# Scores of the first batch element by fp32 matmuls on 32 rows, straight from T

## The reference

```python
Q = einsum('oc,bscm->bsom', Wq, x) + bq      # o = 256 hidden channels
K = einsum('oc,bscm->bsom', Wk, x) + bk
V = einsum('oc,bscm->bsom', Wv, x) + bv
QK = Q^T @ K  over s                           # 256 x 256 for each element and lane
A  = softmax(QK, axis=-1)
out = einsum('bmcC,bmsC->bsCm', A, V)        # only the column sums of A enter
y  = x + Wo out + bo
```

## Time and profile before

| | |
|---|---|
| time, median of three | 199.22 us (196.81 to 209.14) |
| time of the profiled execution | 199.71 us |
| its span | 197.9 us |
| mean granted TensorE clock | 0.911 |
| busy: PE, DVE, ACT, POOL | 165.7, 130.8, 128.8, 99.5 us |
| first exponential of element 0, of element 1 | 31.99 us, 51.63 us |
| first instruction of the last chain after the exponentials | 185.43 us |

### The profile page before, as it was taken

The page is one execution under the profiler, slowest core; times in us unless marked ns, Lnnn a source line. Parts: engine busy times, 40 slices in busy tenths (PEclk is TensorE's granted clock), DMA queues, the critical chain, the costliest instruction groups (busy, mean ns, idle before and its releaser), DMA issues. The chain is left out here.

```text
span 197.9 us, 5954 instructions
## 1 busy us (share of the span) xinstructions
PE 165.7 (84%) x2208; PEld 89.7 (45%) x2208; DVE 130.8 (66%) x291; ACT 128.8 (65%) x529; POOL 99.5 (50%) x122
## 2 busy tenths in 40 slices
PE   0697096999897899999999999989897898799753
PEld 0263035555454545564545455535454453464330
DVE  0355429748886788778777878788778766654241
ACT  0200005957798688788868887988798998874401
POOL 3353656404897299497558755963642303214000
PEclk9999758569999999999999999999999999955975
DMA  5900585893299169639933972588079502200202
GB/s 192 365 6 0 108 196 96 199 239 146 31 199 252 66 131 205 210 62 197 260 137 58 208 206 81 76 196 264 12 128 215 201 0 109 103 6 0 106 5 106
DMA packets 9626, 26.61 MB, mean 134 GB/s; under 512 B 2459, under 2 KB 3326, under 8 KB 9598
## 3 DMA queue, kind: packets, MB, share of 16 engines
q1 hardware_dynamic: 8224, 25.57, 50.1%
q10 hardware_dynamic: 1374, 0.67, 1.3%
HBM read 9.06 MB, written 4.19 MB: 67 GB/s over the span
## 5 line engine op out<-in xcount | busy, mean ns | idle before, releaser
L772 ACT ACTIVATE e_sb<-s_bank,negmax 128x256 f32<-128x256 f32 x256 | 117.6, 495 | 49.6 <-DVE negmax L584 27.9
L584 DVE TENSOR_REDUCE negmax<-s_bank 128x2 f32<-128x512 f32 x128 | 87.1, 686 | 24.4 <-PE s_bank L404 23.1
L404 PE MATMUL s_bank<-stack,wq_st 99*128 99x256 f32 x256 | 63.2, 341 | 3.7 <-ACT e_sb L772 2.5
L404 PEld LDWEIGHTS s_bank<-stack,wq_st 99*128 99x128 f32 x256 | 39.8, 201 | 41.0 <-issue 40.7
L772 ACT ACTIVATION_READ_ACCUMULATOR e_sb<-s_bank,negmax 128x1 f32 x256 | 58.1, 227 | 0.0
L414 PE MATMUL acc<-e_sb,recip 128*32 128x256 f32 x512 | 43.4, 412 | 9.4 <-DVE recip L590 8.9
L815 POOL TENSOR_TENSOR xc<-xs,nm 128x512 f32<-128x512 f32 x15 | 15.9, 1082 | 20.1 <-DVE nm L543 20.1
L866 POOL TENSOR_TENSOR t_parts<-t_sb,t_parts 128x1280 fp32r<-128x1280 f32 x7 | 20.4, 2908 | 4.3 <-DVE t_parts L579 3.8
L565 DVE SCALAR_TENSOR_TENSOR t_sb<-bk_sb,ssum,bz 128x256 f32<-128x256 f32 x28 | 12.9, 465 | 12.4 <-PE bz L382 10.4
L879 POOL TENSOR_TENSOR ws<-wo_sb,aT 128x1024 f32<-128x1024 f32 x7 | 13.4, 1912 | 14.2 <-DVE aT L600 14.2
L414 PEld LDWEIGHTS acc<-e_sb,recip 128*32 128x32 f32 x512 | 10.7, 111 | 20.8 <-DVE recip L590 13.8
(11 more groups left out here) (72 smaller groups left out, 128.8 us busy)
## 6 DMA issues: line engine op xcount, KB each, us to landing
stack<-t_parts SPq DMA_DIRECT2D x32, 256.0 KB, 4.9
xs<-x_rows SPq DMA_DIRECT2D x8, 512.0 KB, 5.7
stack<-t_parts SPq DMA_DIRECT2D x32, 128.0 KB, 4.8
xT<-x_cols SPq DMA_DIRECT2D x8, 512.0 KB, 6.0
y_cols<-yb SPq DMA_DIRECT2D x7, 512.0 KB, 4.1
y_cols<-yb SPq DMA_DIRECT2D x2, 256.0 KB, 2.0
stack<-t_parts SPq DMA_DIRECT2D x8, 32.0 KB
k_sb<-consts ACTq DMA_DIRECT2D x1, 235.5 KB, 4.5
```

Of the source, the lines that this page charges most:

```text
L404: mm = nc.tensor.matmul(s_bank[p % NS][:, CH * h:CH * h + CH], wq_st[:, P * h:P * h + P], stack[:, side, p % Q, p // Q, :], start=True, st ...
L584: nc.vector.tensor_reduce(negmax[:, p % NS, :], s_bank[p % NS][:, :].rearrange("p (h n) -> p h n", h=HC), op=ALU.max, axis=AX.X, negate=Tr ...
L772: last = nc.scalar.activation(e_sb[:, p % NE, h, :], s_bank[p % NS][:, CH * h:CH * h + CH], ACT.Exp, bias=negmax[:, p % NS, h:h + 1], accu ...
```

## The change

Elements 1 to 7 get their scores as before. Element 0 no longer goes through `high_part`, `low_part` and the stack: its scores are fp32 matmuls on the 32 rows of a lane in `t_sb`, with the plain weights `wq_sb` (a new load of 128 KB), and a second matmul on 12 rows adds the bias: `bq_rows` (split bq, picked per t, made by POOL from `bq_sb`, another new load of 128 KB) times `tb_st` (split bias rows in all 128 partitions). Two halves that lie in different row blocks and PSUM banks are issued together: half 1 of lane p and half 0 of lane p + 1. T of element 1 is computed in slots 1 to 5 of element 0, no longer ahead of it, and the statistics of elements 2 and 3 come later too. `gnorm` and `ssum` get two buffers.

```diff
-ANCHOR = {2: 7, 3: 22, 4: 36, **{j: M * (j - 2) + 3 for j in range(5, B)}}
+ANCHOR = {0: 0, 1: 1, 2: 13, 3: 24, 4: 37, **{j: M * (j - 2) + 3 for j in range(5, B)}}
+NEVER = -1000
+HI_FIRST, SPLIT_WQ = 6, 9
 EARLY = {
-    2: {**CHAIN, **dict(gram=-7, variance=-4, read_gram=-6, sum_diagonal=-5, read_variance=-3)},
-    3: {**CHAIN, **dict(sum_rows=-17, mean=-14, gram=-10, sum_groups=-16, read_mean=-13)},
-    4: {**CHAIN, **dict(sum_rows=-18, mean=-15, sum_groups=-17, read_mean=-14)},
+    0: {**dict.fromkeys(CHAIN, NEVER), **dict(t23_product=0, read_t2=0, read_t3=1)},
+    1: {**dict.fromkeys(CHAIN, NEVER), **dict(t01_product=0, tb_product=1, t23_product=3,
+                                              read_t0=1, read_t1=2, read_tb=2, read_t2=3, read_t3=4)},
+    2: {**CHAIN, **dict(sum_rows=-11, mean=-9, gram=-6, variance=-4, sum_groups=-11, read_mean=-9,
+                        read_gram=-5, sum_diagonal=-4, read_variance=-3)},
+    3: {**CHAIN, **dict(sum_rows=-13, mean=-11, gram=-9, variance=-5, sum_groups=-12, read_mean=-10,
+                        read_gram=-7, sum_diagonal=-6, read_variance=-4)},
+    4: {**CHAIN, **dict(sum_rows=-16, mean=-13, gram=-10, sum_groups=-15, read_mean=-12, read_gram=-8, sum_diagonal=-7)},
+    5: {**CHAIN, **dict(sum_rows=-18, sum_groups=-17)},
 }
...
+            def tb_product_first():
+                pe.wait_ge(sblk_done, 1)
+                nc.tensor.matmul(by[:, 0:CH], sblk_first[:, :, :, :].rearrange("p q k t -> p (q k t)"), wk_sb[:, :],
+                                 start=True, stop=True).then_inc(tb_mm, 1)
+
+            def score_first(halves):
+
+                for p, h in halves:
+                    t, q = p // Q, p % Q
+                    pe.wait_ge(t_read, t + 1)
+                    after(pe, exped, p - NS + 1)
+                    rows = slice(C * q, C * q + C)
+                    nc.tensor.matmul(s_bank[p % NS][:, CH * h:CH * h + CH], wq_sb[rows, P * h:P * h + P],
+                                     t_sb[rows, 0, t, :], start=True, stop=False)
+                for p, h in halves:
+                    t, q = p // Q, p % Q
+                    rows = slice(C * q, C * q + NP * T)
+                    mm = nc.tensor.matmul(s_bank[p % NS][:, CH * h:CH * h + CH], bq_rows[rows, t, P * h:P * h + P],
+                                          tb_st[rows, :], start=False, stop=True)
+                    if h == HC - 1:
+                        mm.then_inc(scores, 1)
+
             def score(b, p):
+                if b == 0:
+                    score_first([(p, 1), (p + 1, 0)] if p + 1 < M else [(p, 1)])
+                    return
...
-            sum_rows(2)
-            pe.wait_ge(w_loaded, 16 * 7)
+            pe.wait_ge(w_loaded, 16 * 8)
             t_product(0, 0, t01_mm, bz)
-            tb_product(0)
-            t_product(0, 2, t23_mm, t23_bank(0))
+            tb_product_first()
             gram_of(1)
-            mean(2)
+            pe.wait_ge(bq_done, 1)
+            pe.wait_ge(tb_split, 2)
+            score_first([(0, 0)])
+            score(0, 0)
+            score(0, 1)
             variance(1)
-            t_product(1, 0, t01_mm, bz)
-            tb_product(1)
-            t_product(1, 2, t23_mm, t23_bank(1))
-            pe.wait_ge(set_dve, 2)
-            for p in range(AHEAD):
-                score(0, p)
+            score(0, 2)
```

More of the change, by code:

```diff
@@ L81, in shape_constants, with build @@
     k[p, PAIR + p // (2 * C)] = 1.0
+    k[p % C // T == 1, BLO] = -1.0
+    k[p % C // T == 2, TLO] = -1.0
+    for t in range(T):
+        k[p % C == 0 * T + t, PICKT + t] = 1.0
+        k[p % C == 1 * T + t, PICKT + t] = 1.0
+        k[p % C == 2 * T + t, PICKT + t] = 1.0
     return k
-def build(nc, x_rows, x_cols, wq_stack, wk_rep, bk_rep, wv, wo, bv, bo_rep, consts, y_cols):
+def build(nc, x_rows, x_cols, wq_stack, wq_rep, bq_rep, wk_rep, bk_rep, wv, wo, bv, bo_rep, consts, y_cols):
     f32 = mybir.dt.float32
@@ L112, in build @@
         wk_sb = sb("wk_sb", [P, CH])
+        wq_sb = sb("wq_sb", [P, CH])
+        bq_sb = sb("bq_sb", [P, CH])
+        bq_hi = sb("bq_hi", [P, CH], f32r)
+        bq_st = sb("bq_st", [P, CH], f32r)
+        bq_rows = sb("bq_rows", [P, T, CH], f32r)
         bk_sb = sb("bk_sb", [P, CH])
@@ L280, in bias @@
                     sp.dma_start(dst.bitcast(f32), src.bitcast(f32)).then_inc(bias_stacked[side], 16)
[L282 to L298, removed]
+                for q in range(Q):
+                    high(q)
+                bias(0)
+                sp.wait_ge(parts_done, j)
+                bias(1)
+                for q in range(Q):
+                    low(q)
             def store(j):
@@ L306, in _ @@
                 load_rows(j)
-            stack_up(0)
+            load_cols(0)
             stack_up(1)
-            load_cols(0)
             for b in range(B):
@@ L381, in t_product @@
                         rows = slice(C * q, C * q + C)
-                        mm = nc.tensor.matmul(dst[rows, CH * i:CH * i + CH], gnorm[rows, first + i, :],
+                        mm = nc.tensor.matmul(dst[rows, CH * i:CH * i + CH], gnorm[rows, j % 2, first + i, :],
                                               wk_sb[rows, :], start=True, stop=True)
@@ L412, in column_sums @@
                         after(pe, acc_read, b)
+                    if b == 0 and t == 0:
+                        pe.wait_ge(vare_done, 2)
                 for q in range(Q):
@@ L638, in element @@
                         invert(n // T, n % T)
+                    if slot == HI_FIRST:
+                        high_part(1)
+                    if slot == SPLIT_WQ:
+                        split_wq()
                     if b >= 3 and p == 0:
@@ L900, in _ @@
             column_means(1)
-            pool.wait_ge(w_loaded, 16 * 7)
-            for h in range(HC):
-                last = nc.gpsimd.tensor_scalar(wobv[:, h], wo_sb[:, h, :], bv_sb[:, h:h + 1], 0.0, ALU.mult, ALU.add)
-            last.then_inc(set_pool, 1)
             diagonal(1)
@@ L908, in _ @@
             scaled_sums(1)
+            pool.wait_ge(w_loaded, 16 * 8)
+            for h in range(HC):
+                last = nc.gpsimd.tensor_scalar(wobv[:, h], wo_sb[:, h, :], bv_sb[:, h:h + 1], 0.0, ALU.mult, ALU.add)
+            last.then_inc(set_pool, 1)
             centre_rows(2)
             column_means(2)
+            diagonal(2)
             low_part(1)
-            diagonal(2)
             power(2)
```

158 lines of the change are left out of this document (93 added, 65 removed).

## The result

The changed kernel takes 216.68 us, the median of four runs (215.91 to 217.10), against 200.3 for the kernel before on the same chip: ratio 1.0938, 95% interval 1.0812 to 1.1065. It is slower by 9%, where 197.0 was forecast and 203.5 was the upper end of the range. The profiled execution took 215.91 us with a span of 214.1, 16.2 more than before.

What follows compares the result with a forecast made beforehand. PE was taken as the bound. Slot 14 at 17.7 + 26.1 + 1.7 + 2.5 = 48.0 gained 3.4 us, less 1.2 in element 1: 199.7 - 2.2 = 197.5, 197.0 by the median; range 192.0 to 203.5.

Steps and rivals of the forecast that it cites:

- The head start: Start of the kernel: first score at 17.7 in place of 29.48, 11.8 us earlier, bounds 17.2 and 18.7.
- The price of a lane: Element 0's new scores on PE: 0.85 us a lane, from 0.65 with row blocks overlapping to 1.29 without.
- rival 2: Element 0's scores: row blocks sharing columns run one after the other, a lane 1.29 to 1.35, about 204 us; chance 0.15.
- The worse case: Element 0's scores: weight loads and matmuls hide one another badly, so a lane costs up to 1.29 us.
- The clock: PE up to slot 14: nearly gapless work from 13.4 on, 1.7 us lost at 1.2 GHz, bounds 0 and 5.
- a sign of being wrong: Element 0: the forecast is wrong if the granted clock stays at 0.5 throughout it.
- The work sum: PE work at 2.4 GHz from the first score to slot 14's column sums: 26.1 us, against 16.5 before.
- Slot 14: Column sums that release element 1's first exponential: done at 48.0 against 51.4, 3.4 us gained.
- the wait for the stack: PE before element 1's first score, slot 13: waits 2.5 us for the stack copies, 0 to 4.
- after that: Element 1: 2.3 us more PE work behind slot 14, half counted as 1.2 us, bounds 0 and 2.3.
- the gaps of before: Element 1 before: 3.3 us of PE gaps, waits through ACT and DVE, expected to absorb part of the moved work.

Runs made afterwards that it cites:

- e3_start: Changed kernel with 8, 1, 2 and 1 unused constant matmuls filling PE's gaps before the first score; 214.06 us against 200.36.
- e15: Kernel before, behind real-data matmul streams: A 32-row pairs with 12-row pairs; B, C add one, two short matmuls; E 128 rows, one short. Clock high in A, E; falls in B, C.
- e9: Changed kernel with e7's edits, element 0's main score matmuls on 128 rows (zero weights outside the lane) and PE's start filled; 205.94 us against 201.28.
- e7: Changed kernel with the split of wq moved to the start and POOL's low part of element 2 behind element 3's scaled sums; 214.37 us, ratio 1.0777.
- e8_all: Changed kernel with e7's edits, four lanes at once in element 0 and PE's start filled with unused matmuls; 208.63 us, ratio 1.0502.
- e11_quads_held: e8_all with unused constant matmuls also filling PE's waits in element 0; 203.29 us against 201.28.
- e12: Kernel before with only the change's slots for the statistics and T of elements 2 to 7, no new scores; ratio 1.0370.
- e17: e9 with earlier statistics of elements 2 to 4 and POOL doing element 3's scaled Gram matrix before element 2's high and low parts; 202.69 us, ratio 1.0292.
- e14: Kernel before with unused matmuls filling PE's start and its waits before scores of lanes 1 to 3 of element 0; 192.85 us, ratio 0.9674.
- e13: Kernel before, behind a gapless constant-tile stream of 128-row matmuls, 32-row pairs and fours; clock high from 7.4 to 109.8, 40 pairs or 40 fours 17.5 us each.
- e1: Changed kernel with element 0's main score matmuls on 128 rows, weights zero outside the lane's 32; 222.45 us against 200.36.

## Why the prediction was wrong, point by point

**The head start was nearly right.** First score forecast for 17.7, measured 18.65, at the upper bound (18.7); first exponential forecast near 20.7, measured 21.88, 10.1 us ahead of before. The first load landed 0.5 us later (PE starts at 5.77 against 5.24). The second loads cost little: `t_product(0, 0)` starts at 14.10, 0.3 us later than before (13.81).

**The price of a lane was nearly right.** I took 0.85 (0.65 to 1.29). At 2.4 GHz a lane takes 0.66 (e3_start), the lower end, in a gapless stream 0.555 with its bias pair (e15). The row blocks overlap, and rival 2 (serial row blocks) falls. It gave a time on the right side, 204, for a reason that isn't so; that is luck. The rule from the Trainium skill (TensorE: Matmul & The Clock Gate, "LDWEIGHTS (loading the stationary operand)"), by which I had estimated 0.64 for six weight loads, can't be told from full overlap by the 0.66; in the stream a lane has its six loads in 0.555, less than 0.64, so there they overlap at least in part. The worse case that I built on it, loads and matmuls hiding one another badly, didn't come.

**The step that failed is "The clock".** I wrote "I take 1.7 us lost at 1.2 GHz; bounds 0 and 5", arguing that a PE without gaps is granted the high clock. I even named a clock of 0.5 through element 0 as a sign of being wrong, but gave it neither a price nor a chance. The work sum was sound: 26.1 less 15 lanes x (0.85 - 0.67) is 23.4, and from the side of e9, 34.75 - 16 x (1.37 - 0.67) is 23.5. PE took 43.10 for it, so by this estimate the clock took some 19.7 us, twelve times the term and four times its bound. The Trainium skill (the same page, "What's actually happening") says that the clock is set by how busy PE has been recently; measured against this case's trace that is too little, since PE was busy 43.10 of 44.55 us, 38.83 of 39.00 in e7 and all of the 31.00 in e15's stretch B, all at 1.2 GHz. What PE does while busy matters: matmuls on part of the rows mixed with short ones let the clock fall (e15 B and C), and element 0 of the change has that mix. That the mix is the cause in the kernel itself is carried over from the stream; what the kernels show is that pairs have a low clock with PE full (e3, e7) and 128 rows a high one (e9). The trace of before held a hint that I read as a remnant of the idle start: 0.50 at 40 to 42.5 with PE busy 2.50 of 2.50, in the midst of ten microseconds at 0.50 with PE busy 9.64 of 10.24.

**Slot 14, by terms.** Forecast 48.0, measured 63.2: first score +0.95, clock +18.0 (19.7 - 1.7), lanes -2.7 (26.1 - 23.4), idle places +1.45, and the wait for the stack -2.5, which wasn't there, as a PE at half speed gave the copies their time. These are +15.2. The size of the wait stays open: 2.70 in e8_all is close, but with four lanes at once and a low clock, and e11_quads_held has 1.27.

**Element 1, "after that".** I counted 1.2 us, bounds 0 and 2.3, for PE work moved in. Measured: 4.05, and 1.4 more in element 2. PE was busy 4.43 us longer in element 1 (20.45 against 16.02) and idle 0.38 less (2.90 against 3.28). So the gaps took in nothing: the 2.3 us moved in were paid in full, and 3.41 us at the low clock (76.72 to 80.13) cost up to 1.7 more. I had counted on the gaps of before and costed the moved steps on PE, not on POOL's queue: with T of element 2 later, its high and low part (1.25 + 2.91) hold up `power` of element 3, and a wait of 2.00 us stands where the gaps of before were. e12 shows the same wait with no new score in the kernel. With the order changed in e17, element 1 is still 3.6 us longer than before, all of it busy time of PE (19.97).

**The balance of the span.** First exponential of element 1 +11.77 (-10.11 head start, +21.88 in element 0), element 1 +4.05, element 2 +1.39, element 3 -0.73, the rest -0.28: +16.2.

**Had the clock been held.** e9, e11 and e17, in which it was held through all or nearly all of element 0, stand at 205.9, 203.3 and 202.7, and the kernel before with its clock held at 192.9. So the low clock explains most of the loss of 9%, but no version with it held is faster than before, and element 0 also carries the statistics that stood ahead of it before. The pairs themselves with a held clock were not run in the whole kernel. The nearest is e17, with the same order of halves at 1.37 a lane in place of 0.66, so its 202.7 should be an upper bound; what the change is worth at 2.4 GHz isn't known.

## What to carry to other kernels

Take PE's work at the low clock as one of the cases whenever a change puts matmuls on part of the rows beside short ones, however full PE will be; and read the clock from the duration of an operation whose two levels are known, not from a busy share. When a step is moved, go through the queue of each engine that it touches, and ask what now stands ahead of the next statistic there. Before speeding up a stage at its start, try filling matmuls in PE's waits: here 22 of them, up to the first scores, were worth 3.3% without any change to the work (e14).

## What the runs showed of the hardware

- PE busy 100% by the profile, without a wait, at a granted clock of 0.50 for 31 us (e15, B), and at 1.00 with the short matmul left out (A) or the main ones on 128 rows (E).
- Two and four tiles of 32 x 128 that share their columns take the same time, 0.44 us for fp32 on 256 columns (17.5 us for 40 of either, e13).
- The cast of 99 x 256 to fp32r on DVE took 0.28 us before and 1.75 (after) and 1.72 (e1) beside an operation of 2.9 us on POOL; in e1 it ended at 51.24, when that one did (51.10). What it waits for inside wasn't tested by itself.
- In the kernel before, PE busy 9.64 of 10.24 us at 0.50 (32.99 to 43.23), with scores on 99 rows; with filling ahead of those scores the clock was high there (e14).
- A window that lies before the first recorded change of the clock shows 1.00, whatever the clock was (18.65 to 63.20 after).
